# Attention features in two matmul passes with folded squares, and a new order of projections and features

## The chip, the core and the metric

The kernel runs on one core of one Trainium2 chip. The metric is the device time of one execution, in microseconds, lower is better. TensorE (PE) multiplies matrices into PSUM, VectorE (DVE), ScalarE (ACT) and GpSimd (POOL) work on rows of up to 128 partitions, SyncE (SP) issues DMAs. Each engine runs its own program in order; they meet only at semaphores.

## What is computed

One layer of a graph transformer on 1250 nodes of width 1024, fp32 in and out: a graph convolution over 20000 edges, an attention over all nodes with random features, and a mixture of 8 experts of which each node takes 2. The change is in the attention:

```python
def _apply_kernel(x, orf):               # x: 16 heads, 1250 rows, 64 wide; orf: 256 x 64
    m, d_k = orf.shape
    proj = jnp.einsum('bhld,md->bhlm', x, orf) / d_k ** 0.25
    norm = jnp.sum(x * x, axis=-1, keepdims=True) / (2.0 * math.sqrt(d_k))
    return (jnp.exp(proj - norm) + EPS) / math.sqrt(m)
q, k, v = split(x @ Wq.T + bq), split(x @ Wk.T + bk), split(x @ Wv.T + bv)
q_phi, k_phi = _apply_kernel(q, orf), _apply_kernel(k, orf)
kv = jnp.einsum('bhlm,bhld->bhmd', k_phi, v)
ksum = jnp.sum(k_phi, axis=2)
num = jnp.einsum('bhlm,bhmd->bhld', q_phi, kv)
den = jnp.einsum('bhlm,bhm->bhl', q_phi, ksum)
out = num / den[..., None]
```

## The kernel before

The phases follow one another: the graph part (0 to about 417 us), the attention over eight pairs of heads (to about 1057 us), its output projection, the routing and the experts. fp32 values are split into a rounded high part (`F32R`) and the rest, and the products of the parts are added up in PSUM.

A pair of heads has 128 channels, which are the partitions of its projections. A projection is three thirds of 418, 416 and 416 nodes, each 24 matmuls (`project`, L1570 to L1572) into PSUM banks 0 to 2. The order is keys, values, queries (`wi` 0, 1, 2). Seven pairs run in a loop (`pairs`), the eighth behind it; in the loop the keys of the next pair are projected at the end of a pair. `hw` holds the split weights; GpSimd splits those of the next pair (`split_head`, L691 a cast, L693 a subtraction) as soon as the projection that used the same place is done.

ScalarE moves a third of keys or queries from PSUM into `qf` with its bias (L961), squares it into `sqf` and rounds the squares into `sk`. VectorE (`stack`, L1225 to L1236) rounds `qf` into `tk` and subtracts for the low halves of `tk` and `sk`: for each head, 64 partitions hold the high part and the other 64 the rest. A feature group on TensorE is three passes: `tk` by `orfh` (the rounded random matrix), `tk` by `orfl` (its rest), `sk` by `negr` (minus ones, which sums the squares). For keys a group is two tiles of 128 nodes (`key_features`, six matmuls of 256 columns), for queries one half of the 256 features by a third of the nodes (`query_features`, three matmuls). Groups go to banks 3 and 4 in turn, so a group waits for the exponential of the last but one. ScalarE takes the exponential, VectorE adds the epsilon (L1248, L1261). TensorE transposes the values (L1583), VectorE copies them into `vt` (L1243); `key_values` multiplies keys by values (L1606, 40 matmuls, it needs all five additions and all four copies), `outputs` multiplies the queries by that (L1629), VectorE divides (L1268, L1270) into `att`, TensorE turns it in four parts (`turn`, L1660) through banks 6 and 7, VectorE copies each part into `attnT` (L1278).

In the loop the two turns of parts 0 and 1 stand behind the first third of the next keys, those of parts 2 and 3 behind the second. VectorE's order there is copy 0, `stack` of third 0, copies 1 and 2, `stack` of third 1, copy 3, `stack` of third 2.

## Time and profile before

| | us |
|---|---|
| median of three runs | 1548.04 (1545.38 to 1548.82) |
| the profiled execution | 1546.44 |
| its span | 1544.9 |
| TensorE busy | 1418.7 (92%) |
| VectorE busy | 739.7 (48%) |
| ScalarE busy | 493.8 (32%) |
| GpSimd busy | 410.8 (27%) |

The chain of work that ended last is 77% TensorE. Mean granted TensorE clock over the span is 0.971 of full speed. A row of a timeline is the start and duration in us, the engine, its line, the operation, what it writes and reads, and in brackets how long the engine had been idle and what released it. Matmuls overlap: the distance from one start to the next is what one costs, not its duration. A row by stretch has the stretch and its length, then for TensorE, its weight loads, VectorE, ScalarE and GpSimd the busy time and the number of instructions, then the granted clock, the DMA share and GB/s.

### The profile page before, as it was taken

How to read it: one execution, taken by the hardware profiler on the slowest of the kernel's cores; microseconds unless marked ns; L12 is line 12 of the kernel's file. 1: busy time of each engine (PE TensorE's matmuls, PEld its weight loads, DVE VectorE, ACT ScalarE, POOL GpSimd, SP SyncE). 2: the span in 40 equal slices, each digit the busy share in tenths (PEclk: the TensorE clock that was granted, in tenths of full speed). 3: DMA queues.
4: the chain of work that ended last, by engine and by line, in shares of the span. 5: the costliest groups of instructions: out<-in, count | busy, mean ns of one | idle time of the engine just before them, and what ended most of it. 6: DMA issues, size and time to landing. Idle time of an engine off the chain costs nothing.

```text
span 1544.9 us, 26450 instructions
## 1 busy us (share of the span) xinstructions
PE 1418.7 (92%) x8459; PEld 1237.5 (80%) x8460; DVE 739.7 (48%) x1471; ACT 493.8 (32%) x821; POOL 410.8 (27%) x408
## 2 busy tenths in 40 slices
PE   5798898999999999999999999997999589999996
PEld 2465676799999999999999999996888468777785
DVE  7855334336255444545444445344554514444641
ACT  7411332222033333334332324243123113344531
POOL 7421423344320101010101011002324223333432
PEclk9999999999999999999999999998999579999998
DMA  4100111255410000000000000003242826666852
GB/s 156 46 28 34 58 42 58 69 175 148 116 42 15 27 14 27 14 27 14 27 14 19 22 14 14 0 1 113 67 148 97 323 62 203 202 197 201 266 153 56
DMA packets 58101, 127.79 MB, mean 83 GB/s; under 512 B 7626, under 2 KB 28826, under 8 KB 58048
## 3 DMA queue, kind: packets, MB, share of 16 engines
q1 hardware_dynamic: 48016, 96.79, 18.2%
q0 software_dynamic: 10032, 30.30, 8.2%
q8 instruction: 32, 0.52, 0.1%
q14 instruction: 21, 0.17, 0.0%
HBM read 91.46 MB, written 37.43 MB: 83 GB/s over the span
## 4 chain that ended last, share of the span: by engine, by line
PE 77%; DMA 6%; DVE 6%; issue 5%; ACT 3%; SPq 1%; POOL 1%; DVEq 1%; POOLq 0%; ACTq 0%
PE PB L1570 7%; PE PB L1572 7%; PE PB L1571 7%; PE PB L1472 7%; PE PB L1606 5%; PE PB L1629 5%; PE PB L1748 3%; PE PB L1749 3%; PE PB L1751 3%; DMA ebb<-expert_b 3%; PE PB L1554 2%; PE PB L1513 2%; PE PB L1556 2%; PE PB L1555 2%; PE PB L1515 2%
## 5 line engine op out<-in xcount | busy, mean ns | idle before, releaser
L1570 PE MATMUL PB<-xh,hw 128*128 128x416 f32 (+1 forms) x576 | 204.8, 355 | 0.0
L1572 PE MATMUL PB<-xh,hw 128*128 128x416 f32 (+1 forms) x576 | 203.0, 352 | 0.0
L1571 PE MATMUL PB<-xl,hw 128*128 128x416 f32 (+1 forms) x576 | 202.8, 352 | 0.0
L1472 PE MATMUL PB<-ohs,ohd 128*128 x534 | 121.5, 357 | 35.6 <-issue 22.1
L1748 PE MATMUL PB<-mwh,mth 128*128 128x512 f32 x368 | 149.1, 405 | 5.1 <-DVE mwl L1430 3.5
L691 POOL CAST hw<-hraw 128x1024 fp32r<-128x1024 f32 x24 | 25.1, 1047 | 454.7 <-PE PB L1572 450.2
L1749 PE MATMUL PB<-mwl,mth 128*128 128x512 f32 x368 | 144.7, 393 | 0.0
L1472 PEld LDWEIGHTS PB<-ohs,ohd 128*128 x534 | 52.6, 99 | 101.6 <-issue 84.0
L1751 PE MATMUL PB<-mwh,mtl 128*128 128x512 f32 x368 | 114.2, 392 | 0.0
L1131 DVE TENSOR_SCALAR ohd<-iota,dc 128x128 f16 x178 | 55.2, 310 | 117.0 <-PE PB L1472 101.3
L1571 PEld LDWEIGHTS PB<-xl,hw 128*128 128x128 f32 x576 | 108.7, 189 | 1.3
L1570 PEld LDWEIGHTS PB<-xh,hw 128*128 128x128 f32 x576 | 108.6, 189 | 1.3 <-ACT qf L961 0.2
L1572 PEld LDWEIGHTS PB<-xh,hw 128*128 128x128 f32 x576 | 108.6, 189 | 1.2
L1133 DVE TENSOR_SCALAR ohs<-iota,sc 128x1280 f16 x178 | 106.3, 597 | 0.0
L1541 PE MATMUL PB<-hh,AT 128*128 128x256 f32 x400 | 98.3, 287 | 3.0 <-DVE hr L1147 2.3
L1542 PE MATMUL PB<-hr,AT 128*128 128x256 f32 x400 | 97.5, 285 | 0.0
L961 ACT ACTIVATE qf<-PB,biasT 128x416 f32<-128x416 f32 (+1 forms) x48 | 29.2, 609 | 208.1 <-PE PB L1572 167.2
L1513 PE MATMUL PB<-wqh,xh 128*128 128x256 f32 x320 | 92.5, 289 | 3.3 <-DVE xl L1140 1.7
L1515 PE MATMUL PB<-wqh,xl 128*128 128x256 f32 x320 | 91.2, 285 | 0.0
L1514 PE MATMUL PB<-wql,xh 128*128 128x256 f32 x320 | 91.2, 285 | 0.0
L1748 PEld LDWEIGHTS PB<-mwh,mth 128*128 128x128 f32 x368 | 69.7, 189 | 20.1 <-issue 6.6
L1751 PEld LDWEIGHTS PB<-mwh,mtl 128*128 128x128 f32 x368 | 69.5, 189 | 15.5
(264 smaller groups left out, 3092.9 us busy)
## 6 DMA issues: line engine op xcount, KB each, us to landing
mraw<-expert_w SPq DMA_DIRECT2D x64, 512.0 KB, 8.5
count_rests<-ATf POOLq DMA_DIRECT2D x9, 640.0 KB, 3.3
xrow<-x SPq DMA_DIRECT2D x40, 128.0 KB, 2.9
y_scratch<-xrow SPq DMA_DIRECT2D x40, 128.0 KB, 2.0
yrow<-y_scratch SPq DMA_DIRECT2D x20, 256.0 KB, 2.9
x2n_half<-xhat SPq DMA_DIRECT2D x20, 256.0 KB, 2.4
out<-x SPq DMA_DIRECT2D x9, 512.0 KB
ATf<-wg SPq DMA_DIRECT2D x32, 128.0 KB, 2.2
```

What stands on the lines that cost most here:

```text
L1133: v.tensor_scalar(ohs[:, ds(2 * side + p, 1), :].rearrange("p a n -> p (a n)"), iota[:, :], sc[:, ds(col, 1)], None, ALU.is_equal).then_in ...
L1472: ins = mm(PB[:, 1536 * s + c0:1536 * s + c0 + n], ohd[:, ds(2 * side + p, 1), :].rearrange("p a n -> p (a n)"), ohs[:, ds(2 * side + p, 1 ...
L1513: mm(o, xh[:, k, at], wqh[q % 2][:, k, :], start=(k == 0), stop=False)
L1515: ins = mm(o, xl[:, k, at], wqh[q % 2][:, k, :], start=False, stop=(k == KT - 1))
L1541: mm(o, AT[:, b, at], hh[:, q % 2, b, :], start=(b == 0), stop=False)
L1542: ins = mm(o, AT[:, b, at], hr[:, q % 2, b, :], start=False, stop=(b == TT - 1))
L1570: mm(bank(i, n), hw[:, wi, 0, k, :], xh[:, k, c0:c0 + n], start=(k == 0), stop=False)
L1571: mm(bank(i, n), hw[:, wi, 0, k, :], xl[:, k, c0:c0 + n], start=False, stop=False)
L1572: ins = mm(bank(i, n), hw[:, wi, 1, k, :], xh[:, k, c0:c0 + n], start=False, stop=(k == KT - 1))
L1748: mm(y[c], mth[:, k, :], mwh[par][:, k, c * CW:(c + 1) * CW], start=(k == 0), stop=False)
L1749: mm(y[c], mth[:, k, :], mwl[par][:, k, c * CW:(c + 1) * CW], start=False, stop=False)
L1751: ins = mm(y[c], mtl[:, k, :], mwh[par][:, k, c * CW:(c + 1) * CW], start=False, stop=(k == KT - 1))
```

## The change

Two passes take the place of three. `nk` holds, for each head, 64 partitions of the rounded rows and 64 of squares; `orfn` holds the rest of the random matrix on the former and minus ones on the latter. The first pass is `tk` by `orfh` as before, the second `nk` by `orfn`. For the squares to fit in 64 partitions, ScalarE squares each third in four instructions on 32 partitions, VectorE adds the two halves of a head (32 sums), rounds them and subtracts for the rest. The product of the low rows and the low matrix is no longer formed. ScalarE now rounds the rows into `tk`, VectorE rounds them again into `nk`. The squares have two buffers, so ScalarE waits for the third before last.

The order is new on all engines: the first three key groups stand between the thirds of the values' projection, the rest between the transposes of the values and the thirds of the queries; the second head's product of keys and values is cut in two halves with a query group between; the query features stand inside the next pair's key projection (`between`); all four turns come together at the end of a pair, ahead of the values' projection. `KEYS_OVER` and `KEYS_NEED` are how far the features must be before a third of `tk` and `nk` is overwritten, and how many thirds a key group reads.

```diff
--- before.py
+++ after.py
@@ -25,6 +25,9 @@
...
+KEYS_OVER = (0, 0, 0, 7, 9, 10)
+VALUE_TILES = ((0, 3), (3, 3), (6, 2), (8, 2))
+KEYS_NEED = (1, 2, 2, 3, 3)
...
@@ -744,15 +748,19 @@
...
-            g.memset(negr[:, :].bitcast(F32), -1.0).then_inc(a_cst, 1)
+            g.memset(orfn[:, :, :].bitcast(F32), -1.0).then_inc(a_cst, 1)
...
-            g.memset(sk[:, :, N:NP].bitcast(F32), 0.0).then_inc(a_cst, 1)
+            g.memset(nk[:, :, N:NP].bitcast(F32), 0.0).then_inc(a_cst, 1)
+            g.memset(chunk[:, 1:3, :], 0.0).then_inc(a_cst, 1)
+            g.memset(more_squares[:, :, :], 0.0).then_inc(a_cst, 1)
...
-            pool.wait_ge(a_cst, 6)
-            g.tensor_tensor(orfl[:, :], qf[:, 0:M], orfh[:, :].bitcast(F32), ALU.subtract).then_inc(a_cst, 1)
+            pool.wait_ge(a_cst, 8)
+            g.tensor_tensor(orfn[0:64, 0], qf[0:64, 0:M], orfh[0:64, :].bitcast(F32), ALU.subtract).then_inc(a_cst, 1)
+            g.tensor_tensor(orfn[64:128, 1], qf[64:128, 0:M], orfh[64:128, :].bitcast(F32), ALU.subtract).then_inc(a_cst, 1)
+            pool.wait_ge(a_cst, 10)
...
@@ -956,19 +964,29 @@
                 act.wait_ge(proj_done, 6 + 9 * j + 3 * wi + i % 3 + 1)
                 act.wait_ge(t_done, START + 6 * j + i)
                 act.wait_ge(sq_ready, START + 6 * j + i)
-                act.wait_ge(s_done, START + 6 * j + i)
                 apart(act)
                 a.activation(qf[:, 0:n], bank(i % 3, n), ACT.Identity,
                              bias=biasT[:, wi, ds(j, 1)]).then_inc(qf_ready, 1)
                 act.wait_ge(qf_ready, 3 + 6 * j + i + 1)
-                a.activation(sqf[:, 0:n], qf[:, 0:n], ACT.Square, scale=SQ_SCALE).then_inc(sq_ready, 1)
-                act.wait_ge(sq_ready, START + 6 * j + i + 1)
-                act.wait_ge(phi_done, START + 22 * j + (10 if i >= 3 else 0))
-                a.activation(sk[0:64, 0, c0:c0 + n], sqf[0:64, 0:n], ACT.Copy)
-                a.activation(sk[64:128, 1, c0:c0 + n], sqf[64:128, 0:n], ACT.Copy).then_inc(s_hi, 1)
+                act.wait_ge(phi_done, START + 22 * j + KEYS_OVER[i])
+                a.activation(tk[0:64, 0, c0:c0 + n], qf[0:64, 0:n], ACT.Copy)
+                a.activation(tk[64:128, 1, c0:c0 + n], qf[64:128, 0:n], ACT.Copy).then_inc(t_hi, 1)
+                one, two = squares[i % 2]
+                act.wait_ge(s_done, START + 6 * j + i)
+                a.activation(one[64:96, 0:n], qf[0:32, 0:n], ACT.Square, scale=SQ_SCALE)
+                a.activation(two[64:96, 0:n], qf[32:64, 0:n], ACT.Square, scale=SQ_SCALE)
+                a.activation(one[0:32, 0:n], qf[64:96, 0:n], ACT.Square, scale=SQ_SCALE)
+                a.activation(two[0:32, 0:n], qf[96:128, 0:n], ACT.Square, scale=SQ_SCALE).then_inc(sq_ready, 1)
             def pair(j, last):
+                def key_exp(h, i):
+                    f = 5 * h + i
+                    act.wait_ge(kv_done, START + 2 * j + h)
+                    act.wait_ge(phi_done, START + 22 * j + f + 1)
...
                 act.wait_ge(aux_done, START + 12 * j)
                 for i in range(3):
@@ -977,17 +995,17 @@
...
-                for i in range(3, 6):
-                    project(j, i, 2)
+                    key_exp(0, i)
+                for i in range(3, TT // 2):
+                    key_exp(0, i)
+                for i in range(2):
+                    key_exp(1, i)
+                project(j, 3, 2)
+                for i in range(2, 4):
+                    key_exp(1, i)
+                project(j, 4, 2)
+                key_exp(1, 4)
+                project(j, 5, 2)
...
@@ -1217,43 +1235,67 @@
...
             def stack(j, i):
                 c0, n = THIRDS[i % 3]
                 dve.wait_ge(qf_ready, 3 + 6 * j + i + 1)
-                dve.wait_ge(phi_done, START + 22 * j + (10 if i >= 3 else 0))
-                v.tensor_copy(tk[0:64, 0, c0:c0 + n], qf[0:64, 0:n])
-                v.tensor_copy(tk[64:128, 1, c0:c0 + n], qf[64:128, 0:n]).then_inc(t_hi, 1)
+                dve.wait_ge(phi_done, START + 22 * j + KEYS_OVER[i])
+                v.tensor_copy(nk[0:64, 0, c0:c0 + n], qf[0:64, 0:n])
+                v.tensor_copy(nk[64:128, 1, c0:c0 + n], qf[64:128, 0:n])
                 dve.wait_ge(t_hi, 6 * j + i + 1)
                 v.tensor_tensor(tk[64:128, 0, c0:c0 + n], qf[0:64, 0:n], tk[0:64, 0, c0:c0 + n].bitcast(F32), ALU.subtract)
                 v.tensor_tensor(tk[0:64, 1, c0:c0 + n], qf[64:128, 0:n], tk[64:128, 1, c0:c0 + n].bitcast(F32),
                                 ALU.subtract).then_inc(t_done, 1)
-                dve.wait_ge(s_hi, 6 * j + i + 1)
-                v.tensor_tensor(sk[64:128, 0, c0:c0 + n], sqf[0:64, 0:n], sk[0:64, 0, c0:c0 + n].bitcast(F32), ALU.subtract)
-                v.tensor_tensor(sk[0:64, 1, c0:c0 + n], sqf[64:128, 0:n], sk[64:128, 1, c0:c0 + n].bitcast(F32),
+                one, two = squares[i % 2]
+                dve.wait_ge(sq_ready, START + 6 * j + i + 1)
+                v.tensor_tensor(one[0:96, 0:n], one[0:96, 0:n], two[0:96, 0:n], ALU.add).then_inc(s_hi, 1)
+                dve.wait_ge(s_hi, 2 * (6 * j + i) + 1)
+                v.tensor_copy(nk[64:96, 0, c0:c0 + n], one[64:96, 0:n])
+                v.tensor_copy(nk[0:32, 1, c0:c0 + n], one[0:32, 0:n]).then_inc(s_hi, 1)
+                dve.wait_ge(s_hi, 2 * (6 * j + i) + 2)
+                v.tensor_tensor(nk[96:128, 0, c0:c0 + n], one[64:96, 0:n], nk[64:96, 0, c0:c0 + n].bitcast(F32), ALU.subtract)
+                v.tensor_tensor(nk[32:64, 1, c0:c0 + n], one[0:32, 0:n], nk[0:32, 1, c0:c0 + n].bitcast(F32),
                                 ALU.subtract).then_inc(s_done, 1)
...
+                def key_eps(h, i):
+                    dve.wait_ge(exp_done, 2 + 22 * j + 5 * h + i + 1)
+                    v.tensor_scalar(kphi[:, 2 * i:2 * i + 2, :], kphi[:, 2 * i:2 * i + 2, :], EPS_PHI, None,
+                                    ALU.add).then_inc(kph_ready, 1)
+                def keep_values(i):
+                    t0, nt = VALUE_TILES[i]
...
+                def keep_products(h):
...
+                dve.wait_ge(kv_done, START + 2 * j)
+                for i in range(3):
+                    key_eps(0, i)
+                keep_values(0)
+                key_eps(0, 3)
+                keep_values(1)
+                key_eps(0, 4)
+                keep_values(2)
+                keep_values(3)
+                keep_products(0)
+                for i in range(2):
+                    key_eps(1, i)
+                stack(j, 3)
+                for i in range(2, 4):
+                    key_eps(1, i)
+                stack(j, 4)
+                key_eps(1, 4)
+                stack(j, 5)
+                keep_products(1)
...
@@ -1271,13 +1313,14 @@
                                         rec[:, :].rearrange("p (t a) -> p t a", a=1).broadcast_to([P, 5, DK]),
                                         ALU.mult).then_inc(aux_evac, 1)
-                for i, (t0, nt) in enumerate(((0, 3), (3, 3), (6, 2), (8, 2))):
-                    if not last and i % 2 == 1:
-                        stack(j + 1, i // 2)
+                if not last:
+                    stack(j + 1, 0)
+                for i, (t0, nt) in enumerate(VALUE_TILES):
                     dve.wait_ge(aux_done, START + 12 * j + 8 + i + 1)
                     v.tensor_copy(attnT[:, ds(j, 1), t0 * P:(t0 + nt) * P].rearrange("p a n -> p (a n)"),
                                   bank(6 + i % 2, nt * P)).then_inc(aux_evac, 1)
                 if not last:
+                    stack(j + 1, 1)
                     stack(j + 1, 2)
             for i in range(3):
@@ -1556,27 +1599,39 @@
...
+                    if between and k < KT - 1:
+                        between(k)
...
+                def key_features(h, i):
+                    f = 5 * h + i
+                    pe.wait_ge(exp_done, 22 * j + f + 1)
+                    pe.wait_ge(t_done, START + 6 * j + KEYS_NEED[i])
+                    pe.wait_ge(s_done, START + 1 + 6 * j + KEYS_NEED[i])
+                    for q in range(2):
+                        at = slice((2 * i + q) * P, (2 * i + q + 1) * P)
+                        o = bank(3 + f % 2)[:, q * M:(q + 1) * M]
+                        mm(o, tk[:, h, at], orfh[:, :], start=True, stop=False)
+                        ins = mm(o, nk[:, h, at], orfn[:, h], start=False, stop=True)
+                    ins.then_inc(phi_done, 1)
...
@@ -1584,28 +1639,18 @@
...
+                def key_values(h, first, last_one):
...
+                    for i in range(first, last_one):
+                        m, t = i // TT, i % TT
+                        n = LAST if t == TT - 1 else P
+                        ins = mm(bank(5)[:, m * (DK + 1):(m + 1) * (DK + 1)], kphi[0:n, t, m * P:(m + 1) * P],
+                                 vt[0:n, t, h, :], start=(t == 0), stop=(t == TT - 1))
+                    if last_one == MH * TT:
+                        ins.then_inc(kv_done, 1)
...
@@ -1613,10 +1658,9 @@
...
-                    pe.wait_ge(s_done, START + 6 * j + 4 + (i // 2 if h == 0 else 2))
+                    pe.wait_ge(s_done, START + 1 + 6 * j + 4 + (i // 2 if h == 0 else 2))
...
-                    mm(bank(3 + f % 2, n), orfl[:, m], tk[:, h, c0:c0 + n], start=False, stop=False)
-                    mm(bank(3 + f % 2, n), negr[:, m], sk[:, h, c0:c0 + n], start=False, stop=True).then_inc(phi_done, 1)
+                    mm(bank(3 + f % 2, n), orfn[:, h, m], nk[:, h, c0:c0 + n], start=False, stop=True).then_inc(phi_done, 1)
...
@@ -1630,48 +1674,62 @@
                                      qphi[:, m, t * P:(t + 1) * P], kvs[:, h, m, :], start=(m == 0), stop=(m == MH - 1))
                     ins.then_inc(aux_done, 1)
...
+                def turn(i):
+                    t0, nt = VALUE_TILES[i]
+                    pe.wait_ge(aux_evac, 12 * j + 8 + i + 1)
+                    for q in range(nt):
+                        ins = nc.tensor.transpose(bank(6 + i % 2)[:, q * P:(q + 1) * P], att[:, t0 + q, :], ident[:, :])
+                    ins.then_inc(aux_done, 1)
+                for i in range(3):
+                    project_third(j, 1, i)
                     key_features(0, i)
+                turn_values(0)
+                key_features(0, 3)
+                turn_values(1)
+                key_features(0, 4)
+                turn_values(2)
                 key_features(1, 0)
...
+                turn_values(3)
+                key_values(0, 0, MH * TT)
+                key_features(1, 1)
+                project_third(j, 2, 0)
+                key_features(1, 2)
+                key_features(1, 3)
+                project_third(j, 2, 1)
+                key_features(1, 4)
+                project_third(j, 2, 2)
+                key_values(1, 0, TT)
+                query_features(0, 0)
+                key_values(1, TT, MH * TT)
+                query_features(0, 1)
+                if last:
+                    for i in range(2, 6):
+                        query_features(0, i)
+                    query_features(1, 0)
+                else:
+                    project_third(j + 1, 0, 0, lambda k: query_features(0, 2 + k // 4) if k % 4 == 2 else None)
+                    project_third(j + 1, 0, 1, lambda k: query_features(0, 4 + k // 4) if k % 4 == 2 else None)
+                    query_features(1, 0)
                 pe.wait_ge(kv_evac, START + 2 * j + 1)
                 outputs(0, 0)
                 query_features(1, 1)
                 outputs(0, 1)
...
+                if last:
+                    for i in range(2, 5):
+                        query_features(1, i)
+                else:
+                    project_third(j + 1, 0, 2, lambda k: query_features(1, 2 + k // 2) if k % 2 == 1 else None)
+                query_features(1, 5)
                 pe.wait_ge(kv_evac, START + 2 * j + 2)
                 outputs(1, 0)
                 outputs(1, 1)
...
+                for i in range(4):
+                    turn(i)
+            for i in range(3):
+                project_third(0, 0, i)
```

VectorE at the end of a pair in the loop, before: `attnT` is the copy of a turned part, `tk` and `sk` belong to the next pair's first key third.

```order
L1270 TENSOR_TENSOR kphi<-PB,rec 128x5x64
...
L1278 COPY attnT<-PB 128x384
...
L1227 CAST tk<-qf 64x418
L1228 CAST tk<-qf 64x418
...
L1230 TENSOR_TENSOR tk<-qf,tk 64x418
...
L1234 TENSOR_TENSOR sk<-sqf,sk 64x418
...
L1278 COPY attnT<-PB 128x384
```

The same place of the changed kernel, where `chunk` holds `qf` and one buffer of squares:

```order
L1312 TENSOR_TENSOR kphi<-PB,rec 128x5x64
...
L1245 CAST nk<-chunk 64x418
...
L1248 TENSOR_TENSOR tk<-chunk,tk 64x418
...
L1253 TENSOR_TENSOR chunk<-chunk 96x418
...
L1255 CAST nk<-chunk 32x418
...
L1258 TENSOR_TENSOR nk<-chunk,nk 32x418
...
L1320 COPY attnT<-PB 128x384
```

The first copy of a turned part has moved from ahead of the third to behind it, and the third has nine instructions where it had six.

VectorE in the changed kernel from the last query third but one to the product of the second head; `kphi` is the addition of the epsilon, `kvs` the copy of the product.

```order
L1245 CAST nk<-chunk 64x416
...
L1253 TENSOR_TENSOR chunk<-chunk 96x416
...
L1258 TENSOR_TENSOR nk<-chunk,nk 32x416
...
L1266 TENSOR_SCALAR kphi<-kphi 128x512
...
L1245 CAST nk<-chunk 64x416
...
L1278 COPY kvs<-PB 128x130
```

Before, all five additions of the second head stood ahead of the three query thirds; now the last one stands behind the second of them.

## Rows read from the trace of the kernel before

**Rows 1.** Busy time by stretch, 560 to 640 us; one core.
```profile
560.00:640.00 80.00, 78.11 (x494) 74.30 (x492) 39.22 (x77) 27.56 (x50) 10.25 (x6) 1.00 0.06 20
```

**Rows 2.** TensorE's timeline, one turn of the loop: start, us, what, idle before.
```profile
604.12 0.82 PE L1583 MATMUL PB<-ident,qphi 128*128 128x128 f32 x6
...
606.14 0.28 PE L1594 MATMUL PB<-orfl,tk 128*128 128x256 f32 x1
606.26 0.28 PE L1595 MATMUL PB<-negr,sk 128*128 128x256 f32 x1
...
611.44 4.67 PE L1606 MATMUL PB<-vt,kphi 128*128 128x65 f32 x40 [0.52 <-DVE kphi L1248]
...
619.36 0.35 PE L1570 MATMUL PB<-xh,hw 128*128 128x418 f32 x1
...
632.99 4.57 PE L1606 MATMUL PB<-vt,kphi 128*128 128x65 f32 x40
637.37 0.43 PE L1617 MATMUL PB<-tk,orfh 128*128 128x418 f32 x1
...
651.04 4.57 PE L1629 MATMUL PB<-kvs,qphi 128*128 128x65 f32 x40
655.43 0.44 PE L1570 MATMUL PB<-xh,hw 128*128 128x418 f32 x1
...
684.06 0.81 PE L1583 MATMUL PB<-ident,qphi 128*128 128x128 f32 x6
```

**Rows 3.** Waits of TensorE's weight loads over the eight pairs: total, times, longest.
```profile
PEld PB L1617 <- ACT qphi L997: 16.3, 33, 0.8
```

**Rows 4.** VectorE's timeline in the same turn.
```profile
609.22 0.43 DVE L1248 TENSOR_SCALAR kphi<-kphi 128x512 f32<-128x512 f32 x1 [0.53 <-ACT kphi L987]
...
625.08 0.37 DVE L1227 CAST tk<-qf 64x418 fp32r<-64x418 f32 x1 [4.47 <-ACT qf L961]
...
625.88 0.59 DVE L1230 TENSOR_TENSOR tk<-qf,tk 64x418 fp32r<-64x418 f32 x1
...
627.70 0.59 DVE L1235 TENSOR_TENSOR sk<-sqf,sk 64x418 fp32r<-64x418 f32 x1
...
655.88 0.49 DVE L1270 TENSOR_TENSOR kphi<-PB,rec 128x320 f32<-128x320 f32 x1
660.72 0.56 DVE L1278 COPY attnT<-PB 128x384 f32 x1 [4.34 <-PE PB L1660]
...
665.90 0.42 DVE L1278 COPY attnT<-PB 128x256 f32 x1 [0.87 <-PE PB L1660]
```

**Rows 5.** ScalarE's timeline, one third of the queries.
```profile
624.44 0.61 ACT L961 ACTIVATE qf<-PB,biasT 128x418 f32<-128x418 f32 x1 [4.29 <-PE PB L1572]
625.08 0.56 ACT L964 ACTIVATE sqf<-qf 128x418 f32<-128x418 f32 x1
625.67 0.55 ACT L968 ACTIVATE sk<-sqf 64x418 fp32r<-64x418 f32 x1
```

**Rows 6.** GpSimd (POOL) and VectorE (DVE) timelines where they overlap, and GpSimd's first fill.
```profile
633.40 1.04 POOL L691 CAST hw<-hraw 128x1024 fp32r<-128x1024 f32 x1 [25.36 <-PE PB L1572]
634.52 2.36 POOL L693 TENSOR_TENSOR hw<-hraw,hw 128x1024 fp32r<-128x1024 f32 x1
...
634.68 2.43 DVE L1228 CAST tk<-qf 64x416 fp32r<-64x416 f32 x1
...
423.84 0.31 POOL L747 MEMSET negr<- 128x256 f32 x1 [2.86 <-DMA y_scratch<-resty]
...
433.99 2.41 POOL L693 TENSOR_TENSOR hw<-hraw,hw 128x1024 fp32r<-128x1024 f32 x1
...
434.18 2.67 DVE L1230 TENSOR_TENSOR tk<-qf,tk 64x416 fp32r<-64x416 f32 x1
```

**Rows 7.** Busy time and granted clock by stretch, in the graph part.
```profile
364.10:367.60 3.50, 1.77 (x13) 1.36 (x11) 2.35 (x6) 1.02 (x2) 0.62 (x1) 1.00 0.37 119
367.60:371.00 3.40, 3.40 (x16) 3.19 (x16) 1.02 (x3) 0.00 (x0) 0.97 (x2) 0.51 0.55 138
```

More of the change, by code:

```diff
@@ L123, in gps_layer @@
         tk = keep("tk", [P, 2, NP], F32R, pb)
-        sk = keep("sk", [P, 2, NP], F32R, pb)
+        nk = keep("nk", [P, 2, NP], F32R, pb)
         qphi = keep("qphi", [P, MH, NP], F32, pb)
@@ L129, in gps_layer @@
         vt = keep("vt", [P, TT, 2, DK + 1], F32, pb)
-        qf = keep("qf", [P, CW], F32, pb)
-        sqf = keep("sqf", [P, CW], F32, pb)
+        chunk = keep("chunk", [P, 3, THIRDS[0][1]], F32, pb)
+        qf = chunk[:, 0, :]
         pb.close()
@@ L183, in gps_layer @@
         kvs = keep("kvs", [P, 2, MH, DK + 1], F32, pa)
+        more_squares = keep("more_squares", [P, 2, THIRDS[0][1]], F32, pa)
         rec = keep("rec", [P, TT // 2], F32, pa)
+        squares = ((chunk[:, 1, :], chunk[:, 2, :]), (more_squares[:, 0, :], more_squares[:, 1, :]))
         orfh = keep("orfh", [P, M], F32R, pa)
-        orfl = keep("orfl", [P, M], F32R, pa)
-        negr = keep("negr", [P, M], F32R, pa)
+        orfn = keep("orfn", [P, 2, M], F32R, pa)
         pa.close()
@@ L636, in _ @@
             pool.sem_inc(aux_evac, 2)
[L638 removed]
+            for signal in (rest_taken, rest_over, a_w, t_done, s_done, s_done, sq_ready, phi_done, kv_done, aux_done, kv_evac,
                            mt_trans, y_free):
@@ L1557, in row_tile, with project_third @@
                 ins.then_inc(r.done, 1)
-            def project(j, wi, after=None):
+            def project_third(j, wi, i, between=None):
+                c0, n = THIRDS[i]
                 pe.wait_ge(a_w, START + 3 * j + wi + 1)
-                for i, (c0, n) in enumerate(THIRDS):
-                    if wi == 0:
-                        pe.wait_ge(qf_ready, 6 * j + i + 1)
-                    elif wi == 1:
-                        pe.wait_ge(qf_ready, 3 + 6 * j + i + 1)
-                    else:
-                        pe.wait_ge(vt_ready, 3 * j + i + 1)
-                    for k in range(KT):
-                        mm(bank(i, n), hw[:, wi, 0, k, :], xh[:, k, c0:c0 + n], start=(k == 0), stop=False)
-                        mm(bank(i, n), hw[:, wi, 0, k, :], xl[:, k, c0:c0 + n], start=False, stop=False)
-                        ins = mm(bank(i, n), hw[:, wi, 1, k, :], xh[:, k, c0:c0 + n], start=False, stop=(k == KT - 1))
-                    ins.then_inc(proj_done, 1)
-                    if after:
-                        after(i)
@@ L1577, in pair @@
-            def pair(j, last):
-                project(j, 1)
-                for i, (t0, nt) in enumerate(((0, 3), (3, 3), (6, 2), (8, 2))):
+                if wi == 0:
+                    pe.wait_ge(qf_ready, 6 * j + i + 1)
+                elif wi == 1:
+                    pe.wait_ge(qf_ready, 3 + 6 * j + i + 1)
+                else:
+                    pe.wait_ge(vt_ready, 3 * j + i + 1)
+                for k in range(KT):
+                    mm(bank(i, n), hw[:, wi, 0, k, :], xh[:, k, c0:c0 + n], start=(k == 0), stop=False)
+                    mm(bank(i, n), hw[:, wi, 0, k, :], xl[:, k, c0:c0 + n], start=False, stop=False)
+                    ins = mm(bank(i, n), hw[:, wi, 1, k, :], xh[:, k, c0:c0 + n], start=False, stop=(k == KT - 1))
+                    if between and k < KT - 1:
+                        between(k)
@@ L1602, in key_values @@
                     pe.wait_ge(aux_evac, 2 + 12 * j + 4)
-                    for m in range(MH):
-                        for t in range(TT):
-                            n = LAST if t == TT - 1 else P
-                            ins = mm(bank(5)[:, m * (DK + 1):(m + 1) * (DK + 1)], kphi[0:n, t, m * P:(m + 1) * P],
-                                     vt[0:n, t, h, :], start=(t == 0), stop=(t == TT - 1))
-                    ins.then_inc(kv_done, 1)
+                    for i in range(first, last_one):
[5 more added lines that the diff above has]
+                        ins.then_inc(kv_done, 1)
                 def query_features(h, i):
@@ L1654, in pair @@
                 outputs(1, 1)
-                def turn(i):
-                    t0, nt = ((0, 3), (3, 3), (6, 2), (8, 2))[i]
-                    pe.wait_ge(aux_evac, 12 * j + 8 + i + 1)
-                    for q in range(nt):
-                        ins = nc.tensor.transpose(bank(6 + i % 2)[:, q * P:(q + 1) * P], att[:, t0 + q, :], ident[:, :])
-                    ins.then_inc(aux_done, 1)
-                if last:
-                    for i in range(4):
-                        turn(i)
-                else:
-                    def turns(i):
-                        for q in range(2 * i, min(2 * i + 2, 4)):
-                            turn(q)
-                    project(j + 1, 0, turns)
-            project(0, 0)
-            pe.wait_ge(a_cst, 7)
+                for i in range(4):
+                    turn(i)
+            for i in range(3):
+                project_third(0, 0, i)
             pairs(pe, pair)
```

53 lines of the change are left out of this document (8 added, 45 removed).

## The prediction

> **What bounds the kernel now.** I read the busy time by stretch first: in 80 us of the middle of the attention part TensorE is busy for 78.11 us at full clock, VectorE for 39.22 and ScalarE for 27.56 [rows 1]. So TensorE bounds this part, and what counts is its matmuls and the moments in which it stands. Next I read TensorE's timeline over one turn of the loop over head pairs [rows 2]. The transposes of the values start at 604.12, and one turn later at 684.06: a turn takes 79.94 us. A feature matmul of 256 columns follows its neighbour by 0.12 us (606.14 and 606.26), and the 72 matmuls of one projection run from 619.36 to 632.99, 13.63 us or 0.19 each. The 40 matmuls of keys by values take 632.99 to 637.37, 4.38 us; the 40 of one head's outputs take 651.04 to 655.43, 4.39.
>
> From these the turn without any standing: three projections 40.9, 60 key feature matmuls at 0.12 7.1, 36 query feature matmuls at 0.19 6.8, two products of keys and values 8.8, outputs of two heads 8.8, 20 transposed tiles at 0.11 (4.38 / 40) 2.2: 74.6 us. The other 5.3 us are waits: from 604.12 to 611.44 lie 7.3 us in which only 10 transposes and 36 feature matmuls run (5.4), and the query features stand for ScalarE's exponentials, 16.3 us in the eight pairs [rows 3].
>
> **What goes.** Two matmuls where there were three: 20 of 0.12 and 12 of 0.19 per pair, 2.4 + 2.3 = 4.7 us. With the features set between projection thirds the exponentials have time to finish, so I let all 5.3 us of old waits go too. A turn would be 79.9 - 4.7 - 5.3 = 69.9 us if nothing new waited.
>
> **What is added.** Per third of a projection VectorE has nine instructions for six, ScalarE seven for four. VectorE: four copies of 0.37 and five two-input operations of 0.59 [rows 4], 4.45 us, with the gaps between instructions 4.65. ScalarE: 0.61 for the eviction, 0.55 for each of two roundings and four squares [rows 5], 3.9 us. The squares work on 32 partitions, which no row shows. Between 0.55 (128 partitions take 0.56 and 64 take 0.55, so partitions don't count) and 0.14 (a quarter) I take 0.55. Over six thirds that is 28 us of VectorE and 23 of ScalarE in a turn, both under the bound. What matters is where VectorE, which works in order, has a third to prepare ahead of something that TensorE waits for. There are three such places.
>
> **Place 1, the end of a pair.** Zero is TensorE's first output matmul of the second head (651.04). TensorE ends the outputs at +4.4, VectorE the division of their second half at +5.3 (655.88 and 0.49) [rows 2, 4]. VectorE then prepares the next keys' first third, 4.65 us, to +10.0, and only then copies the first turned tiles, 0.56, to +10.55. TensorE has done two of the four turns; the third needs that copy's bank. It turns at +10.6 and again behind the second copy (+11.1), and begins the values' projection at +11.5. The 10 transposes alone would have it there at +5.5. Wait: 6.0 us. Before, this copy stood ahead of the third and a projection third lay between the turns.
>
> **Place 2, after the values' projection.** Zero is its end (604.12). GpSimd splits the next weights from +0.4: a cast of 1.04 and a subtraction of 2.36, to about +3.9 [rows 6]. VectorE's third addition of the key epsilon is ready at +1.6 and falls into the subtraction. A copy that met one took 2.43 us in place of 0.37 [rows 6] and ended 0.23 after it; so +4.15. All value copies now stand behind it: copy 0.56 (+4.7), addition 0.43, copy, addition, two copies of 0.42 [rows 4], +7.05. TensorE needs all of them for keys by values. Its own work there is 16 feature matmuls and 10 transposes, 3.0 us. Wait: 4.1 us; 2.2 if GpSimd held nothing up.
>
> **Place 3, ahead of the second head's keys by values.** Zero is the end of the queries' second third. ScalarE needs 0.5 + 0.61 + 1.13 + 2.24 to the squares, +4.5; VectorE adds (+5.1), copies twice (+5.9), subtracts twice (+7.1), and then adds the last epsilon, +7.6. TensorE is there at +5.1 (0.5 of features, 4.6 of projection): a wait of 2.5. But GpSimd begins its split at +5.5, while VectorE copies. A two-input operation that met its subtraction took 2.67 us for 0.59 [rows 6]. 
>
> A turn then takes 69.9 + 6.0 + 4.1 + 4.5 and 0.5 for first matmuls behind short waits: 85.0 us, 5.1 more than now, 36 us in seven turns.
>
> **The clock.** Half busy for 3.5 us (1.77 busy), TensorE ran the next 3.4 us at 0.51 of its clock, the 1.2 GHz level, with 16 matmuls where 30 fit [rows 7]: 14 of 0.12 us lost, 1.6 us. In the loop now the clock is 1.00. Places 1 and 3 stand for longer than that row, place 2 in pieces. I count 4.0 us a turn (two falls and half of a third), 28 us in seven turns. The Trainium skill (TensorE: Matmul & The Clock Gate, The HAM clock gate) calls the low clock the default state that activity lifts. If it falls at each wait the loop pays twice for it.
>
> **Around the loop.** The last pair has no place 1 and no weights to split: it gives back about 3.4 us of feature matmuls and exponential waits, and pays the short forms of places 2 and 3 and perhaps one fall, +1. At the start GpSimd fills 256 + 2 x 836 more columns (0.31 us for 256, [rows 6]) and subtracts in two instructions, +2.6 us ahead of the first eviction; the later first key thirds hold TensorE. Between 0, since TensorE is in its projections then, and 5, I take 3.
>
> Sum, against the profiled execution's own 1546.4 us: + 36 + 28 + 1 + 3 = 1614. The median shown is 1.6 above that execution: 1616.
>
> **Rivals.**
> - The waits come, the clock stays high. For it: the feature matmuls and transposes in places 1 and 2 keep TensorE from being idle throughout. Against it: [rows 7]. 1546.4 + 36 + 4 = 1586, about 1588.
> - The waits are at their long ends and each fall costs 2.4 us (a second low stretch). 7 x (6.1 + 7.2) + 4 = 97, about 1643.
> - The other side: only place 1 remains, because VectorE keeps GpSimd out at its thirds and the value copies and the last epsilon get there in time. A turn is then 69.9 + 6.0 + 0.5 = 76.4, 3.5 less than now; seven turns give 24, the last pair 5, the start takes 3: 1546.4 - 26 = 1520, about 1522. It decides where the new waits of a turn are below 79.9 - 70.4 = 9.5 us. Against it: place 3 has 2.5 us even without GpSimd, and place 2 2.2.
> - The change doesn't do what it says for the work of VectorE: the small operations cost less than a full one, thirds take about 3.5 us, and the waits come to just about 9.5: no change, 1546.
>
> **Chances.** Forecast 48%, clock high 27%, long ends 9%, about no change 5%, faster 11%. About 0.2%, 3 us, is what a measurement can tell. Slower: the first three and 2 of the 5 that lie around no change, 0.86; same: the other 3, 0.03; faster 0.11. The range 1562 to 1652 takes in the first three with their spread and leaves 1546 and 1522 outside. Within the forecast itself 1595 to 1635.
>
> **What would show it.** Right: a turn of 85 to 91 us; the third turn's transposes waiting about 5 us for the copy into the attention output, behind the nine operations of a third; keys by values waiting for the epsilon addition by about 4 us, twice a turn, and VectorE operations of more than 1 us beside GpSimd's subtraction; granted clock under 1.00 all through the loop; four feature matmuls per key group. Wrong: TensorE's idle time per turn under 9 us, VectorE's third under 4 us, or a loop at clock 1.00 throughout. The prediction fails in sign if TensorE waits at place 1 alone.

## The result, and the profile after

| | before | after |
|---|---|---|
| median, us | 1546.71 (1542.92 to 1548.82) | 1684.35 (1679.94 to 1686.66) |
| the profiled execution | 1546.44 | 1686.66 |
| its span | 1544.9 | 1685.1 |
| mean granted clock | 0.971 | 0.899 |

The ratio is 1.089 [1.087, 1.091]: slower by 138 us, where I had forecast 68. The page of the changed kernel has the cause in one row. Each digit is a fortieth of the span, TensorE's granted clock in tenths of full speed:

```profile
span 1685.1 us, 26380 instructions
...
PE 1478.5 (88%) x8203; PEld 1302.9 (77%) x8204; DVE 797.3 (47%) x1615; ACT 567.1 (34%) x965; POOL 416.8 (25%) x411
...
PEclk9999999999979788887978788798899859999998
```

TensorE has fewer matmuls (20 + 12 less for each pair) and is busy for 60 us more. The digits of 7 and 8 are the loop over head pairs. What waits there, over the eight pairs (total, times, longest):

```profile
PE PB L1650 <- DVE kphi L1266: 36.1, 7, 5.3
PEld PB L1682 <- DVE attnT L1320: 35.4, 16, 4.8
PE PB L1682 <- DVE attnT L1320: 32.1, 8, 4.5
...
PE PB L1638 <- DVE vt L1272: 11.1, 7, 1.6
```

TensorE's timeline of one turn, from the outputs of a pair's second head to those of the next:

```profile
617.96 4.57 PE L1673 MATMUL PB<-kvs,qphi 128*128 128x65 f32 x40
622.37 0.50 PE L1682 MATMUL PB<-ident,kphi 128*128 128x128 f32 x3
...
628.44 1.15 PE L1682 MATMUL PB<-ident,kphi 128*128 128x128 f32 x4 [4.55 <-DVE attnT L1320]
629.48 0.71 PE L1612 MATMUL PB<-xh,hw 128*128 128x418 f32 x1
...
646.47 0.28 PE L1629 MATMUL PB<-orfh,tk 128*128 128x256 f32 x1
...
651.35 0.56 PE L1638 MATMUL PB<-ident,qphi 128*128 128x128 f32 x2 [1.59 <-DVE vt L1272]
652.42 8.80 PE L1650 MATMUL PB<-vt,kphi 128*128 128x65 f32 x40 [0.52 <-DVE vt L1272]
...
683.87 4.53 PE L1650 MATMUL PB<-vt,kphi 128*128 128x65 f32 x20 [5.07 <-DVE kphi L1266]
...
716.90 4.57 PE L1673 MATMUL PB<-kvs,qphi 128*128 128x65 f32 x40
```

A turn is 98.94 us where it was 79.94 [rows 2]. Three waits stand in it, at the three places of the prediction: at 628.44, at 651 and at 683.87. And a product of 40 matmuls that took 4.38 takes 8.6 (652.42 to about 661). The same turn by stretch, with the granted clock behind TensorE's busy time:

```profile
617.96:716.90 98.94, 86.62 (x461) 0.83 0.05 16
622.40:627.70 5.30, 1.02 (x8) 0.99 0.32 99
627.70:634.50 6.80, 6.06 (x19) 0.50 0.00 0
651.60:665.20 13.60, 13.08 (x56) 0.50 0.11 36
682.30:695.95 13.65, 12.08 (x50) 0.50 0.12 38
```

Behind each wait stands a stretch at 0.50, the 1.2 GHz level: 34 us of each turn. All six turns between 519.20 and 1112.85 have the same three lengths. Before, no stretch of the loop was at low clock ([rows 1] has its middle).

VectorE and GpSimd at the second and the third place:

```profile
646.88 1.04 POOL L695 CAST hw<-hraw 128x1024 fp32r<-128x1024 f32 x1 [25.39 <-PE PB L1614]
...
648.00 2.54 POOL L697 TENSOR_TENSOR hw<-hraw,hw 128x1024 fp32r<-128x1024 f32 x1
...
648.70 2.12 DVE L1266 TENSOR_SCALAR kphi<-kphi 128x512 f32<-128x512 f32 x1
...
679.05 1.22 POOL L695 CAST hw<-hraw 128x1024 fp32r<-128x1024 f32 x1 [28.51 <-PE PB L1614]
679.40 1.31 DVE L1258 TENSOR_TENSOR nk<-chunk,nk 32x416 fp32r<-32x416 f32 x1
680.35 2.56 POOL L697 TENSOR_TENSOR hw<-hraw,hw 128x1024 fp32r<-128x1024 f32 x1
680.73 2.63 DVE L1259 TENSOR_TENSOR nk<-chunk,nk 32x416 fp32r<-32x416 f32 x1
683.39 0.43 DVE L1266 TENSOR_SCALAR kphi<-kphi 128x512 f32<-128x512 f32 x1
```

An addition of 0.43 takes 2.12, a subtraction of 0.59 takes 2.63. Their ends lie 0.3 (650.82 against 650.54) and 0.45 (683.36 against 682.91) behind the end of GpSimd's subtraction. In all, the seven outputs of the loop start at 519.20 to 1112.85, six turns of 98.94. The first starts 28.2 later than before (491.04), and what lies behind the last is 1.9 shorter. Less the 19.0 of the seventh turn, 7.3 us come from outside the loop's turns. These rows can't say which end they belong to: the projection of the next keys, 13.6 us, now stands ahead of the second head's outputs, where it stood behind them [rows 2].

### The profile page after: what moved, and what is told of

Read it like the earlier page. It is cut to its first block, busy times and chain, and to the rows that moved or that the text cites. A ratio compares the mean times of both kernels' runs of the same rounds, so it can differ in the third digit from the quotient of the medians.

```text
span 1685.1 us, 26380 instructions
## 1 busy us (share of the span) xinstructions
PE 1478.5 (88%) x8203; PEld 1302.9 (77%) x8204; DVE 797.3 (47%) x1615; ACT 567.1 (34%) x965; POOL 416.8 (25%) x411
## 4 chain that ended last, share of the span: by engine, by line
PE 71%; DVE 10%; issue 7%; DMA 5%; ACT 3%; SPq 1%; POOL 1%; DVEq 1%; POOLq 0%; ACTq 0%
PE PB L1650 8%; PE PB L1515 6%; PE PB L1612 6%; PE PB L1613 6%; PE PB L1614 6%; PE PB L1673 4%; PE PB L1806 3%; PE PB L1807 3%; PE PB L1809 3%; DMA ebb<-expert_b 2%; PE PB L1556 2%; PE PB L1597 2%; PE PB L1599 2%; PE PB L1557 2%; PE PB L1598 2%
## 5 line engine op out<-in xcount | busy, mean ns | idle before, releaser
L1612 PE MATMUL PB<-xh,hw 128*128 128x416 f32 (+1 forms) x576 | 219.0, 380 | 0.0
L1613 PE MATMUL PB<-xl,hw 128*128 128x416 f32 (+1 forms) x576 | 216.4, 376 | 0.0
L1614 PE MATMUL PB<-xh,hw 128*128 128x416 f32 (+1 forms) x576 | 214.6, 373 | 0.0
L1650 PE MATMUL PB<-vt,kphi 128*128 128x65 f32 (+1 forms) x640 | 134.5, 403 | 42.8 <-DVE kphi L1266 36.1
L1650 PEld LDWEIGHTS PB<-vt,kphi 128*128 128x128 f32 (+1 forms) x640 | 132.7, 317 | 48.3 <-DVE kphi L1266 38.6
L1612 PEld LDWEIGHTS PB<-xh,hw 128*128 128x128 f32 x576 | 119.9, 208 | 3.9 <-issue 1.6
L1613 PEld LDWEIGHTS PB<-xl,hw 128*128 128x128 f32 x576 | 119.2, 207 | 2.1
L1015 ACT ACTIVATE qphi<-PB 128x416 f32<-128x416 f32 (+1 forms) x96 | 48.8, 519 | 212.6 <-PE PB L1663 170.3
L1614 PEld LDWEIGHTS PB<-xh,hw 128*128 128x128 f32 x576 | 118.4, 205 | 2.2
```

The lines of the kernel that those rows point to most:

```text
L1612: mm(bank(i, n), hw[:, wi, 0, k, :], xh[:, k, c0:c0 + n], start=(k == 0), stop=False)
L1613: mm(bank(i, n), hw[:, wi, 0, k, :], xl[:, k, c0:c0 + n], start=False, stop=False)
L1614: ins = mm(bank(i, n), hw[:, wi, 1, k, :], xh[:, k, c0:c0 + n], start=False, stop=(k == KT - 1))
L1650: ins = mm(bank(5)[:, m * (DK + 1):(m + 1) * (DK + 1)], kphi[0:n, t, m * P:(m + 1) * P], vt[0:n, t, h, :], start=(t == 0), stop=(t == TT - 1))
```

## The experiments

All were timed against the kernel before. Its median was 1546.0 beside experiments 1, 2, 3 and 8, 1545.4 beside 4 to 7, and 1548.2 beside 9 and 10. "Us less" means less than the changed kernel's 1684.4, where nothing else is named.

**1. Fill the waits.** Matmuls into a bank that is free at that moment, ahead of the instruction that waits, at all three places. What waits stays as late as it was.

```diff
+def filler(count):   # bank(5) <- xh by xh, 256 columns
...
 for i in range(4):
+    if i == 2 and not last: filler(36)
     turn(i)
...
+pe.wait_ge(kv_evac, START + 2 * j); filler(12)
 turn_values(2)
 ...
+filler(6)
 key_values(0, 0, MH * TT)
...
+pe.wait_ge(kv_evac, START + 2 * j + 1); filler(40)
 key_values(1, 0, TT)
```

> The changed kernel with useless matmuls of 256 columns (rounded node rows by rounded node rows, into the part of PSUM bank 5 that nothing uses) where TensorE waits in each turn of the loop: 36 ahead of the third turned part, 12 and 6 around the last transposes of the values, 40 ahead of the second head's product of keys and values. At 0.12 us each they are a little shorter than the waits that they fill (4.5, 1.6 and 0.5, 5.1 us). Theory (the loop's 99 us a turn are 70 of work, 14 of waits and 14 of low clock): the waits stay, the clock stays high, a turn falls to 85 us and the kernel to 1586 to 1595 us. Rival (the time is all waits, the low clock only goes with them): the turn stays at 99 us and the kernel at about 1684.

Measured 1584.06 (1582.9 to 1586.8), ratio 1.024 [1.022, 1.026]. One turn by stretch:

```profile
560.00:645.20 85.20, 83.22 (x556) 1.00 0.05 18
```

The turn is 85.2 us at clock 1.00. The prediction had 85.0 without the clock. So of the 138 us, 100 (1684.4 - 1584.1) are the low clock. The other 38 are what is left of the waits once the matmuls that went are taken off.

**2. The first place alone:** copies of the turned parts ahead of the third.

```diff
-                if not last:
-                    stack(j + 1, 0)
                 for i, (t0, nt) in enumerate(VALUE_TILES):
...
                 if not last:
+                    stack(j + 1, 0)
                     stack(j + 1, 1)
```

> The changed kernel, VectorE's four copies of the turned parts ahead of the next pair's first key third in place of behind it. Theory: TensorE's wait of 4.5 us for the copy goes, 1.2 us of passing between the engines stays, the fall of the clock there goes too (6.8 us of low clock a turn now), and the first key groups wait under 1 us: a turn loses 4 of wait and 3 of clock, 99 to 92, and the kernel comes to about 1635 us. Rival (the wait only moves to the first key features, which need the third that is now late): under 2 us a turn, 1670 or more.

Measured 1637.2 (1634.4 to 1638.8), ratio 1.058 [1.056, 1.061]: 47 us less, 6.7 a turn. The longest wait for the turned parts' copy fell from 4.8 to 0.6. The forecast of 1635 holds.

**3. The third place alone:** the last epsilon ahead of the second query third, on VectorE, and its exponential ahead on ScalarE.

```diff
-                stack(j, 4)
                 key_eps(1, 4)
+                stack(j, 4)
```

> The changed kernel, the second head's last exponential (ScalarE) and last addition of the epsilon (VectorE) ahead of the second query third in place of behind it. Theory: the wait of 5.1 us before the second product of keys and values goes, and with it the 13.7 us of low clock that follow it: 5 and 7 us of a turn's 99, the kernel at about 1600 us. Rival (the wait moves to the query features, which need the thirds that come later): the product begins on time, but TensorE waits at the first or third query group, and the kernel stays above 1650.

Measured 1584.96 (1583.1 to 1585.6), ratio 1.025 [1.023, 1.027]: 99 us less. A turn is 13.5 shorter (98.94 to 85.40), though the wait that went is 5.3. The turn, at a clock of 0.90:

```profile
592.80:678.20 85.40, 78.12 (x461) 0.90 0.05 18
```

I had expected 1600. The two places that are left still have their low clock, but this edit took more than its own: the stretch behind the second place ends after 10.2 us, not 13.65. The gains of single places don't add up.

```profile
627.10:637.30 10.20, 10.20 (x45) 0.50 0.00 0
```

**4. GpSimd's share alone.** The split of the next values' weights waits for the first head's additions, that of the queries' for the second head's.

```diff
                 for i in range(3):
+                    if i:
+                        pool.wait_ge(kph_ready, 10 * j + 5 * i)
                     split_head(j + 1, i)
```

> The changed kernel (1684.4) with one thing else: GpSimd starts the split of the next pair's values' weights only after the first head's fifth epsilon addition, and that of the queries' weights after the second head's fifth. Nothing else moves. Theory: GpSimd's subtraction stretched the third epsilon addition to 2.12 us (0.43 alone) and two subtractions of the query third to 1.31 and 2.63 (0.37 and 0.59): 1.7 us off the wait ahead of the first product and 3.0 off the one ahead of the second, 7 x 4.7 = 33: 1651, and less again (to about 1610) where a shorter wait leaves the clock up. Rival: VectorE would then wait for ScalarE's squares instead and the waits stay: 1675 or more.

Measured 1603.05 (1601.8 to 1604.5), ratio 1.038 [1.035, 1.041]: 81 us less, at the low end of what I expected. The waits of the loop:

```profile
PE PB L1684 <- DVE attnT L1322: 32.1, 8, 4.5
...
PE PB L1652 <- DVE kphi L1268: 16.7, 7, 2.4
```

The wait at the third place is 2.4 instead of 5.3; the prediction had 2.5 for it without GpSimd. At the second place the projection ends at 623.26 and the product begins here, at full clock:

```profile
627.43 4.68 PE L1652 MATMUL PB<-vt,kphi 128*128 128x65 f32 x40 [0.56 <-DVE vt L1274]
```

Of the 4.2 us between them 3.0 are TensorE's own work: 1.2 of wait where there were 3.0. Both together are 4.7 us a turn, 33 in seven, as the theory had it; the other 48 of the 81 came from the clock. Not all of it came back. The shorter wait at the third place still has a low stretch behind it (TensorE's timeline, then the stretch):

```profile
650.12 2.72 PE L1652 MATMUL PB<-vt,kphi 128*128 128x65 f32 x20 [2.31 <-DVE kphi L1268]
```

```profile
652.15:662.35 10.20, 10.20 (x40) 0.50 0.16 51
```

So a wait of 2.3 us in front of the product is no safe one.

**5 and 6. What does the place of a wait decide?** The fillers stay at two places, and one is open.

```diff
 # the third place open
-pe.wait_ge(kv_evac, START + 2 * j + 1); filler(40)
 key_values(1, 0, TT)
 # its twin, the first place open
-    if i == 2 and not last: filler(36)
     turn(i)
```

> The kernel with the fillers (matmuls of 256 columns into an unused place, 1584.1 us) keeps its fillers at the first two waits and loses them at the third, the wait of the second head's keys-by-values product (5.3 us). Theory: what a low clock costs hangs on what comes behind the wait. In the changed kernel's profile the low clock lasts 13.65 us from here, through the product of 65-column matmuls; a turn has 34 us at low clock that cost 14.2, so 0.42 us each: 5.7 a turn, 1584 + 7 x 5.7 = 1624 (1615 to 1632). Rival one: every fall costs the 1.6 us that I had taken before, 1595. Rival two: every fall costs the same third of the 14.2, 4.7 a turn, 1617; this one is told apart by the twin kernel whose wait at the turns is open.

> The twin: fillers at the second and third wait, none at the first, the 6.0 us wait of the turned parts, behind which stand transposes and the values' projection (416 columns). Theory (the price hangs on what follows): low for 6.8 us, 0.42 each, 2.9 a turn: 1584 + 20 = 1604 (1598 to 1610), half of what the wait at the product costs, though this wait is the longer one. Rival one: 1.6 a fall, 1595. Rival two: 4.7 whatever follows, 1617, the same as the twin.

Measured: the wait at the product 1630.56 (1629.8 to 1630.8), ratio 1.056 [1.053, 1.058], 46.5 us over the filled kernel. The wait at the turns 1599.46 (1592.4 to 1600.6), ratio 1.034 [1.030, 1.038], 15.4 over it. The first edit also opens a wait of 2.4 us in the last pair, so I compare the turns. Measured from the second head's outputs of one pair to those of the next, a turn of the filled kernel is 85.1 on average (1018.50 - 507.98 over six). With the wait at the product open it is 91.2 (1058.07 - 510.89), 6.1 more; with the wait at the turns open 86.8 (1026.61 - 505.91), 1.7 more. I had expected 5.7 and 2.9. The rival of one price for all is out: the shorter wait (5.3 against 6.0 us) costs over three times as much clock. TensorE behind the open wait at the product (stretch first, then its timeline):

```profile
565.70:582.70 17.00, 14.06 (x56) 0.50 0.09 31
```

```profile
568.63 4.53 PE L1654 MATMUL PB<-vt,kphi 128*128 128x65 f32 x20 [5.28 <-DVE kphi L1266]
572.93 0.69 PE L1666 MATMUL PB<-tk,orfh 128*128 128x418 f32 x1
...
573.77 4.37 PE L1654 MATMUL PB<-vt,kphi 128*128 128x65 f32 x20
...
581.87 0.55 PE L1666 MATMUL PB<-tk,orfh 128*128 128x416 f32 x1
...
582.85 0.35 PE L1613 MATMUL PB<-xl,hw 128*128 128x418 f32 x1
```

The low clock lasts 17 us here, through the whole product and into the projection behind it (matmuls of 418 columns at 0.35 us apart, then 0.19). That is the longest form: three of the eight pairs have it, the other five have 13.65 us, as the changed kernel has. In the twin TensorE has the projection next and is slow for 6.8 us, in one of the seven turns for 10.2:

```profile
599.80:606.60 6.80, 3.41 (x11) 0.50 0.00 0
```

Half of this stretch still lies in the wait: TensorE is busy for 3.41 us, and half of that is the 1.7. In the changed kernel the stretch at this place had 6.06 busy, which by the same halving is an estimated 3.0, and the one at the product 12.08, or 6.0. So the ratio there is about two.

**7. Wide matmuls ahead of the product,** behind the same open wait.

```diff
 pe.wait_ge(kph_ready, 10 * j + 5 * h + 5)
 ...
+if h == 1 and first == 0:
+    filler(32)
 for i in range(first, last_one):
```

> As the kernel with the open wait at the product, but behind that wait, ahead of the product, stand 32 matmuls of 256 columns (3.8 us at full clock, 7 at low clock). Theory: narrow matmuls hold the low clock; with wide ones first it comes back after about 6.8 us and the product runs in 4.4: 3.8 + 2.9 a turn, 1584 + 47 = 1631, with low stretches of 6.8 us. Rival: a wait of this place costs 13.65 us of low clock whatever follows: 3.8 + 5.7 a turn, 1651, with low stretches of 13.65 us.

Measured 1627.96 (1621.9 to 1628.5), ratio 1.053 [1.049, 1.056]: 3 us less than the 1630.6 without them, with 256 matmuls more. A turn is 90.9 (1057.25 - 512.09 over six), 5.8 over the filled kernel's. The wide matmuls take 3.8 of it at full clock, so 1.9 are left for the clock, where experiment 5 paid 6.1. Stretches behind the wait:

```profile
568.10:574.90 6.80, 5.19 (x24) 0.50 0.23 77
574.90:603.20 28.30, 28.30 (x186) 1.00 0.00 0
```

```profile
569.71 6.39 PE L1621 MATMUL PB<-xh 128*128 128x256 f32 x32 [5.07 <-DVE kphi L1266]
575.94 2.34 PE L1656 MATMUL PB<-vt,kphi 128*128 128x65 f32 x20
```

The clock is back after the wide matmuls, and the product runs at full speed. So a wait of the same length at the same place has a low stretch of 3.4 or 6.8 us behind it (four pairs each), or one of 13.65 or 17, by what TensorE does next. What it is about the 40 matmuls of 65 columns (their width, or the weight load that each has) these runs don't tell apart.

**8. All three places mended,** and at the second the first value copy ahead of the third addition.

```diff
+ the edits of 2, 3 and 4, and:
-                for i in range(3):
+                for i in range(2):
                     key_eps(0, i)
                 keep_values(0)
+                key_eps(0, 2)
                 key_eps(0, 3)
```

> The changed kernel with both of these, with VectorE's first copy of the values ahead of the third addition of the epsilon, and with GpSimd's split of the value and query weights held back until the additions of a head are done, so that it does not meet VectorE. Theory: the waits fall under 4 us a turn and the clock stays high: a turn of 73 to 75 us, the kernel at 1500 to 1515 us, faster than before the change. Rival (VectorE's 28 us of preparing thirds hold TensorE wherever they stand): a turn of 80 or more, the kernel at 1550 or above.

Measured 1510.3 (1500.1 to 1514.1), ratio 0.975 [0.971, 0.979]: faster than the 1546.0 of before by 36 us. One turn at clock 1.00 and one with a low stretch left in it:

```profile
574.29:651.34 77.05, 75.17 (x462) 0.96 0.06 20
651.34:725.21 73.87, 72.00 (x461) 1.00 0.06 21
```

**9. The third split later still,** behind VectorE's second query third.

```diff
-                    if i:
-                        pool.wait_ge(kph_ready, 10 * j + 5 * i)
+                    if i == 1:
+                        pool.wait_ge(kph_ready, 10 * j + 5)
+                    if i == 2:
+                        pool.wait_ge(s_done, START + 1 + 6 * j + 5)
```

> The version with the three places mended (1510.3, 1500.1 to 1514.1), and GpSimd's split of the queries' weights held back further, until VectorE has done the second query third. In the mended version it still meets that third: two of VectorE's subtractions take 1.09 and 2.43 us instead of 0.37 and 0.59, 2.6 us of VectorE's time in each turn. Theory: VectorE is hardly waited for there (the waits of query features for its third sum to 4 to 5 us over all eight pairs), so at most 5 us go: 1506 (1500 to 1511). Rival: those 2.6 us also push the copies ahead of later products and the low clock behind them: 2.6 x 7 = 18, 1492.

Measured 1504.28 (1502.6 to 1508.7), ratio 0.972 [0.970, 0.974], the fastest of all. Against the 1510.3 this is 6 us less, inside that kernel's own spread, so the step itself isn't shown. Two turns in the middle of the loop are 73.9 us each at full clock:

```profile
575.24:723.06 147.82, 144.07 (x921) 1.00 0.06 21
```

**10. A third pass put back** into the mended kernel.

```diff
 mm(o, tk[:, h, at], orfh[:, :], start=True, stop=False)
+mm(o, tk[:, h, at], orfh[:, :], start=False, stop=False)
 ins = mm(o, nk[:, h, at], orfn[:, h], start=False, stop=True)
```

> The same mended version with a third matmul in every feature group, of the same shapes as the one that the change removed (it adds the first pass a second time, so the features are other numbers): 32 more matmuls a pair, 12 for the queries and 20 for the keys. Theory: with the waits gone TensorE sets the time, and the two passes are worth what I took in the prediction, 20 x 0.12 + 12 x 0.19 = 4.7 us a pair: 1510 + 8 x 4.7 = 1548, the time of the kernel before; then the whole gain of the change is this one term. Rival: other work hides in TensorE's small waits and the extra passes cost less than half, below 1530.

Measured 1562.15 (1559.0 to 1571.5), ratio 1.007 [1.005, 1.010], 14 above what I expected. Its turn:

```profile
746.79:825.20 78.41, 76.55 (x493) 1.00 0.06 20
```

78.4 against the 73.9 of experiment 8: 4.5 us a turn, close to the 4.7. Before the change a turn was 79.9, so the new order, once mended, is worth the other 1.5. The surplus lies elsewhere. The added pass changes the features and with them, it seems, the routing. The experts take more matmuls, 400 of this group where the mended kernel has 368:

```profile
L1810 PE MATMUL PB<-mwh,mth 128*128 128x512 f32 x400 | 162.5, 406 | 2.9 <-DVE mtl L1450 1.4
```

From the last outputs of the attention to the end it takes 517 us (1049.3 to 1566.7), the kernel of experiment 9 498 (1008.9 to 1507.2). The whole times of the two therefore can't be compared; the turns can.

## Why the prediction was wrong in its size

**Removed, 4.7 us a turn and the old waits 5.3: right.** The third pass is worth 4.5 (experiment 10). The filled kernel's turn of 85.2 less the 14.3 of waits below leaves 70.9, where I had 69.9 and 0.5. In the mended kernel a turn is 73.9. Some 3 us of it are short waits at places 1 and 2.

**Place 1, 6.0 us: right to the tenth.** The projection starts at 629.48, 11.5 behind the first output matmul (617.96), as I had it. The nine operations take 4.6 us (623.21 to 627.79), and the ones on 32 partitions cost as much as those on 64, copies and subtractions alike:

```profile
623.58 0.38 DVE L1246 CAST nk<-chunk 64x418 fp32r<-64x418 f32 x1
623.97 0.59 DVE L1248 TENSOR_TENSOR tk<-chunk,tk 64x418 fp32r<-64x418 f32 x1
...
626.21 0.37 DVE L1256 CAST nk<-chunk 32x418 fp32r<-32x418 f32 x1
626.61 0.59 DVE L1258 TENSOR_TENSOR nk<-chunk,nk 32x418 fp32r<-32x418 f32 x1
```

ScalarE's squares on 32 partitions take 0.55 each, the value that I chose.

**Place 2, 4.1 us: 3.0 measured.** The projection ends at 646.47, the product begins at 652.42, and own work is 3.0. GpSimd's subtraction caught not the third addition but the fourth (648.70): the third and the first value copy got ahead of it. Without GpSimd 1.2 are left (experiment 4), where I had 2.2; its share is 1.8, and I had 1.9.

**Place 3, 4.5 us: 5.3 measured,** at the long end (5.4). VectorE was stretched in two operations, 679.40 and 680.73. The Trainium skill (SBUF — State Buffer, Who interferes with whom) says that whichever starts first holds the port for the whole instruction. The rows agree: GpSimd started at 680.35, VectorE's subtraction at 680.73, and the subtraction ended behind GpSimd's. That VectorE's chain keeps GpSimd out, on which the 2.5 hung, did not come.

The waits sum to 14.3 us where I had 14.6. That this is so close is partly luck: place 2 was 1.1 too long and place 3 0.8 too short. With the clock held up the kernel takes 1584; my rival without a clock term said 1588.

**The clock, "I count 4.0 us a turn": this is the step that failed.** With 69.9 + 14.3 + 0.5 = 84.7, the measured turn of 98.9 leaves 14.2 us, 3.6 times as much; over seven turns that is 99 us where I had 28, and the difference is more than the whole miss of 68. A turn of 85 to 91 us, my sign of being right, did not come. The price of 1.6 a fall came from one low stretch of 3.4 us [rows 7]. (That many us hold 28 matmuls of 0.12, not 30, so the row gave 1.4.) Two things were wrong with it. First, place 2 counted as half a fall. It is a whole one: TensorE was busy for 4.9 of 6.6 us at full clock, and then come the 13.6 us at 0.50 shown above.

```profile
645.00:651.60 6.60, 4.89 (x35) 0.99 0.02 4
```

Second, I took the length of a fall from that one row and not from what TensorE does next. Where the keys-by-values product follows, the low stretch is 13.65 us long and takes the whole product with it; it ends only in the projection behind the product. Where a projection follows at once it is 6.8. Experiments 5 to 7 show that it is what follows that decides. The Trainium skill (TensorE: Matmul & The Clock Gate, HAM oscillation) gives the penalty as half of the throttled time. By that rule, as an estimate, the 34 us a turn would cost up to 17; with some 3 us of them spent waiting anyway, 15.5. The measured 14.2 is a little under it. So the share that a low stretch costs was right, and its length was what I had wrong.

**Around the loop,** I had +3 at the start and +1 in the last pair, 4 in sum; measured 7.3 in sum. Which end has the rest stays open.

Faster was possible with the same arithmetic: with its order mended the change gives 44 us (1548.2 to 1504.3), about three quarters of it from the pass that is gone (4.5 of 6.0 us a turn).

## What to carry to other kernels

When an order makes TensorE wait, price the wait twice: its length, and half of the time at low clock behind it. For the second, look at what stands behind the wait: ahead of a product of narrow matmuls it cost 6.1 us, ahead of a projection 1.7 to 3.0. And where TensorE waits for the last of many small results, VectorE's next batch and GpSimd's next job should both stand behind those results. With that done at all three places the same arithmetic went from 9% slower to 3% faster.

## What the runs showed of the hardware

- The low clock lasted 6.8 us (once in seven turns 10.2) ahead of a projection (418 columns) and 10.2 to 17 us ahead of 40 matmuls of 65 columns. With 32 matmuls of 256 columns put between, it was back before the product.
- A wait of 2.3 us in front of the product still had 10.2 us of low clock behind it (experiment 4).
- In front of the product 5.3 us of wait cost 6.1 us of clock, more than the wait itself; matmuls of no use, run during the waits, took 100 us off the whole kernel.
- Two of GpSimd's jobs, each held back a little, gave 81 us: they had stretched three VectorE instructions a turn.
- VectorE's copies and subtractions of 418 columns take 0.37 and 0.59 us on 32 partitions as on 64.
